# A two-layer spectral convolution on one core: image reloads, sums, differences and inverse adds at other places of the order, and forward stores in half as many transfers

## The reference

```python
# layer 0: real spectrum, one real block weight per channel block of 48
f  = fft2(x, axes=(1, 2), norm='ortho');  Xh = (f.real - f.imag)[:, :, :46]
o2 = relu(Xk @ w1[0] + b1[0]) @ w2[0] + b2[0]          # kept: 23 columns kw
x  = ifft2(pad(softshrink(o2, 0.01)), s=(45, 90)).real + x
# layer 1: complex spectrum, complex block weights
xs = rfft2(x)[:, :, :23];  xr, xi = xs.real, xs.imag
o1r = relu(xr @ w1[0] - xi @ w1[1] + b1[0]); o1i = relu(xi @ w1[0] + xr @ w1[1] + b1[1])
o2r, o2i = softshrink(o1r @ w2[0] - o1i @ w2[1] + b2[0]), softshrink(o1i @ w2[0] + o1r @ w2[1] + b2[1])
y  = irfft2(pad(o2r + 1j * o2i), s=(45, 90)) + x
```

## Time and profile before

| | |
|---|---|
| three runs | 593.26, 598.96, 599.08 us; median 598.96 |
| the profiled execution | 594.54 us, of it 592.6 us from the first to the last instruction (the span) |
| mean granted TensorE clock | 0.947 of full speed |
| PE, DVE, POOL, ACT busy | 81%, 61%, 47%, 36% of the span |
| 16 DMA engines | 108.29 MB, mean 183 GB/s; 73% of their time on the three queues of SP, POOL and ACT |

### The profile page before, as it was taken

The page is one execution under the profiler, slowest core; times in us unless marked ns, Lnnn a source line. Parts: engine busy times, 40 slices in busy tenths (PEclk is TensorE's granted clock), DMA queues, the critical chain, the costliest instruction groups (busy, mean ns, idle before and its releaser), DMA issues.

```text
span 592.6 us, 16944 instructions
## 1 busy us (share of the span) xinstructions
PE 479.6 (81%) x6944; PEld 334.2 (56%) x6944; DVE 361.8 (61%) x728; ACT 211.1 (36%) x485; POOL 276.7 (47%) x267
## 2 busy tenths in 40 slices
PE   1418789998898899798888899699997899997763
PEld 0015568776575667476566566566675666775411
DVE  6625456686576667475747656656776767666532
ACT  1203344544234433253234333254334433443101
POOL 9916542661456424671357523674258522322123
PEclk9999789999998999898997989989999999999958
DMA  8659966364897959794796938968698967633587
GB/s 179 209 115 156 210 150 169 100 176 119 226 239 150 236 144 245 210 219 136 205 256 146 243 100 207 255 151 223 168 236 206 222 188 186 165 106 100 129 222 207
DMA packets 81617, 108.29 MB, mean 183 GB/s; under 512 B 10441, under 2 KB 67903, under 8 KB 81414
## 3 DMA queue, kind: packets, MB, share of 16 engines
q1 hardware_dynamic: 64044, 61.01, 37.7%
q0 software_dynamic: 11024, 40.46, 30.0%
q10 hardware_dynamic: 6474, 5.76, 5.0%
HBM read 53.97 MB, written 53.19 MB: 181 GB/s over the span
## 4 chain that ended last, share of the span: by engine, by line
PE 41%; DMA 24%; DVE 14%; POOL 10%; issue 5%; ACT 2%; SPq 2%; POOLq 0%; DVEq 0%; ACTq 0%
DMA img<-x 20%; PE ps L718 8%; PE ps L667 6%; PE ps L705 6%; PE ps L743 6%; PE ps L624 5%; PE ps L654 5%; DVE img L595 4%; DVE uv L517 4%; POOL y L419 3%; POOL xs L397 3%; DVE ns L571 3%; SPq L327 2%; DMA jr<-scr_i 2%; ACT p L486 2%
## 5 line engine op out<-in xcount | busy, mean ns | idle before, releaser
L411 POOL TENSOR_TENSOR uv<-img 128x768 f32<-128x768 f32 (+1 forms) x48 | 101.6, 2128 | 29.9 <-DMA img<-x 29.5
L419 POOL DMA_DIRECT2D y<-img x56 | 40.1, 718 | 138.7 <-DVE img L595 134.5
L654 PE MATMUL ps<-jr,cst 64*64 64x384 f32 (+1 forms) x736 | 83.7, 518 | 13.8 <-DVE img L595 8.0
L718 PE MATMUL ps<-wt,o 128*64 128x96 f32 x1472 | 78.7, 258 | 19.7 <-DVE o L563 19.3
L667 PEld LDWEIGHTS ps<-cst,bt 128*64 128x64 f32 x1472 | 65.6, 148 | 39.1 <-issue 26.2
L718 PEld LDWEIGHTS ps<-wt,o 128*64 128x64 f32 x1472 | 69.3, 143 | 32.4 <-issue 32.4
L517 DVE TENSOR_TENSOR uv<-img 128x768 f32<-128x768 f32 (+1 forms) x48 | 63.2, 1316 | 37.7 <-DMA img<-x 35.2
L667 PE MATMUL ps<-cst,bt 128*64 128x90 f32 x1472 | 74.5, 259 | 13.8 <-DMA bt<-scr_f 13.8
L595 DVE TENSOR_TENSOR img<-ps,img 109x768 f32<-109x768 f32 x76 | 72.5, 955 | 20.9 <-PE ps L654 20.2
L397 POOL TENSOR_TENSOR xs<-xs,nt 128x360 f32<-128x360 f32 (+1 forms) x48 | 41.6, 867 | 87.3 <-DVE nt L549 66.1
L705 PE MATMUL ps<-xs,wt 64*97 64x180 f32 (+1 forms) x768 | 70.5, 321 | 12.0 <-POOL xs L397 11.7
(11 more groups left out here) (44 smaller groups left out, 456.2 us busy)
## 6 DMA issues: line engine op xcount, KB each, us to landing
y<-img POOLq DMA_DIRECT2D x28, 540.0 KB, 8.0
scr_f<-fs SPq DMA_DIRECT2D x384, 36.0 KB
scr_i<-et SPq DMA_DIRECT2D x48, 288.0 KB, 5.1
jr<-scr_i SPq DMA_DIRECT2D x92, 144.0 KB, 5.7
img<-x POOLq DMA_DIRECT2D x24, 540.0 KB, 9.9
bt<-scr_f SPq DMA_DIRECT2D x40, 288.0 KB, 6.6
y<-img POOLq DMA_DIRECT2D x14, 270.0 KB, 6.8
img<-x POOLq DMA_DIRECT2D x12, 270.0 KB, 5.4
```

The source lines that it names most:

```text
L411: nc.gpsimd.tensor_tensor(uv[n % 2][:, 1, 0:j1 - j0, :], img[t % IMGS][:, j0:j1, 0, :], img[t % IMGS][:, j0:j1, 1, :], ALU.subtract).then_ ...
L654: last = mm(ps[64 * p:64 * p + 64, B0 + a, 0:m], w_inv[c, r, :], set_rows(t, g)[c, p, 0:m], start=True, stop=True)
L718: last = mm(ps[64 * r:64 * r + 64, P2 + p, b * 2 * BS:(b + 1) * 2 * BS], o11[:, b, 2 * p + r, :], w21[:, block_no(s // STEPS, b), :], star ...
```

## The change

The list of `schedule()` is written anew, and the forward part of task 0 is treated apart:

1. **Refills**, in the list of a step before: refill 0 and 1 behind `d0` (steps 5 and 0), refill 2 behind `rows`, refill 3 at the end of step 1. Now: refill 0 and 1 ahead of `d1` and `d0`, refill 2 behind `e` in step 1, refill 3 where refill 2 was.
2. **Sums and differences** (`uv`) come one place later: the first of a step behind `c1`, the second behind `c0`, none at the end of the step before.
3. **Inverse groups** were spread 2, 3, 4 and 3 over steps 3, 4, 5 and 0; the first one now stands at the end of step 2, and steps 3, 4, 5 and 0 have 3 each (after it 1 + 2 in step 3). Chunk 0 ends with group 3, now early in step 4.
4. **The add** of a group is a part of its own. For the group between `d1` and `d0` it stands behind `d0` now, so DVE shrinks layer 0 first. The store of a finished chunk hangs on the add.
5. **Forward stores**: 4 transfers of 72 KB a group in place of 8 of 36 KB, behind both copies.
6. **Forward groups of task 0** use all eight PSUM banks in turn, and DVE copies one of the two banks.

```diff
-            inv[s] = [("inv", t - 1, g) for g in ((0, 1), (2, 3, 4), (5, 6, 7, 8))[i - 3]]
+            inv[s] = [("inv", t - 1, g) for g in ((1, 2), (3, 4, 5), (6, 7, 8))[i - 3]]
+        if i == 2 and 0 < t < TASKS - 1:
+            inv[s] = [None, None, ("inv", t - 1, 0)]
...
-        order += first
+        order += uv[0:1]
+        order += both(groups[0])
         if s > 1:
             order.append(("e", s - 2))
-        order += uv[1:2]
-        order += last[0:1]
+        if i == 1 and t > 1:
+            order.append(("refill", t - 2, 2))
+        order += both(groups[1])
         if s < NSTEPS:
             order.append(("c0", s))
-        if 0 < s <= NSTEPS:
-            order.append(("d1", s - 1))
-        order += last[1:2]
-        if s < NSTEPS:
-            order.append(("d0", s))
+        order += uv[1:2]
         if i == 5 and t > 0:
             order.append(("refill", t - 1, 0))
         if i == 0 and t > 1:
             order.append(("refill", t - 2, 1))
+        if 0 < s <= NSTEPS:
+            order.append(("d1", s - 1))
+        order += both(groups[2])[0:1]
+        if s < NSTEPS:
+            order.append(("d0", s))
+        order += both(groups[2])[1:2]
...
         if i == 1 and t > 1:
-            order.append(("refill", t - 2, 2))
+            order.append(("refill", t - 2, 3))
...
-        order += last[2:3]
-        order += ahead[0:1]
-        if i == 1 and t > 1:
-            order.append(("refill", t - 2, 3))
+        order += both(groups[3])
...
-                    for p in range(2):
-                        sp.wait_ge(f_cp, 2 * n + p + 1)
-                        for a in range(2):
-                            for o in range(2):
-                                sp.dma_start(scr_f[t][o * KWP // 2:(o + 1) * KWP // 2, :, p, g, a].rearrange("k e s c -> (k e) (s c)"),
-                                             fs[k][64 * a + 32 * o:64 * a + 32 * o + KWP, p, :]).then_inc(f_st[k], 16)
+                    sp.wait_ge(*(f_cp, 2 * (n - CH + 1)) if t else (f_act, n + 1))
+                    if t == 0:
+                        sp.wait_ge(f_dve, n + 1)
+                    for a in range(2):
+                        for o in range(2):
+                            sp.dma_start(scr_f[t][o * KWP // 2:(o + 1) * KWP // 2, :, :, g, a].rearrange("k e p s c -> (k e) p (s c)"),
+                                         fs[k][64 * a + 32 * o:64 * a + 32 * o + KWP]).then_inc(f_st[k], 16)
...
+                if kind == "fwd" and what[0] == 0:
+                    g = what[1]
+                    if g >= FS:
+                        dve.wait_ge(f_st[g % FS], 64 * (g // FS))
+                    dve.wait_ge(f_mm, g + 1)
+                    nc.vector.tensor_copy(fs[g % FS][:, 1, :], ps[:, 2 * (g % 4) + 1, 0:2 * HC]).then_inc(f_dve, 1)
...
-                if kind == "inv" and (what[0] < TASKS - 1 or what[1] not in LAST_POOL):
+                if kind == "add" and (what[0] < TASKS - 1 or what[1] not in LAST_POOL):
```

More of the change, by code:

```diff
@@ L120, in schedule, with both @@
 def schedule():
+    def both(group):
+        return [group, ("add",) + group[1:]] if group else []
     order = [("uv", 0, 0), ("uv", 0, 1)]
@@ L141, in schedule @@
         t, i = divmod(s, STEPS)
-        first, last = inv[s][0:len(inv[s]) - 3] if len(inv[s]) > 3 else [], inv[s][max(len(inv[s]) - 3, 0):]
+        groups = [None] * (4 - max(len(inv[s]), 3)) + inv[s]
+        groups += [None] * (4 - len(groups))
         uv = [("uv",) + f[1:] for f in fwd[s]]
-        ahead = [("uv",) + f[1:] for f in fwd[s + 1]] if s + 1 < NSTEPS else []
         if s + 2 < NSTEPS:
@@ L364, in _ @@
                                      scr_i[t][:, :, a, 4 * j:4 * j + 4, :].rearrange("k e h c -> (k e) (h c)")).then_inc(landed, 16)
-                if kind == "inv" and what[0] == TASKS - 1 and what[1] % 2 == 1:
+                if kind == "add" and what[0] == TASKS - 1 and what[1] % 2 == 1:
                     g, (b, f) = what[1] // 2, divmod(TASKS - 1, HALVES)
@@ L412, in _ @@
                                             ALU.subtract).then_inc(v_ok, 1)
-                if kind == "inv" and what[0] < TASKS - 1 and (what[1] + 1) // 2 in [b for a, b in CHUNKS] and what[1] % 2 == 1:
+                if kind == "add" and what[0] < TASKS - 1 and (what[1] + 1) // 2 in [b for a, b in CHUNKS] and what[1] % 2 == 1:
                     t, g = what
@@ L426, in _ @@
                         pool.dma_start(folded(k, p, j0, j1), rows_of(x[b], HR * p + j0, HR * p + j1, f)).then_inc(x_ld[k][c], 16)
-                if kind == "inv" and what[0] == TASKS - 1 and what[1] in LAST_POOL:
+                if kind == "add" and what[0] == TASKS - 1 and what[1] in LAST_POOL:
                     t, (g, r) = what[0], divmod(what[1], 2)
@@ L448, in _ @@
                     if n >= FS:
[L449 removed]
+                        act.wait_ge(f_st[n % FS], 64 * (n // FS))
                     act.wait_ge(f_mm, n + 1)
[L451 to L452 removed]
+                    if t == 0:
+                        nc.scalar.activation(fs[n % FS][:, 0, :], ps[:, 2 * (g % 4), 0:2 * HC], ACT.Copy).then_inc(f_act, 1)
+                    else:
+                        for p in range(2):
+                            nc.scalar.activation(fs[n % FS][:, p, :], ps[:, P3 + p, 0:2 * HC], ACT.Copy).then_inc(f_cp, 1)
                 if kind == "x":
@@ L627, in _ @@
                     for p in range(2):
[L628 removed]
+                        tenant[p] = [(f_cp, 2 * (n - CH) + p + 1)] if t else []
                 if kind == "inv":
```

25 lines of the change are left out of this document (15 added, 10 removed).

## The result

| | before | changed |
|---|---|---|
| median of four runs each | 596.11 us | 619.66 us |
| lowest to highest | 592.52 to 599.08 | 615.47 to 622.20 |
| profiled execution / its span | 594.54 / 592.6 us | 615.47 / 613.7 us |
| mean granted TensorE clock | 0.947 | 0.939 |

The ratio is 1.039, 95% interval 1.029 to 1.049. The forecast was 587 us with a range of 571 to 604: wrong in sign. All ratios in this text leave disturbed runs out on both sides, so a ratio can differ by up to 1.2% from that of the medians beside it. Single runs of one kernel lie within 1.1% of each other in the table; in the later sets of 13 runs the kernel before lies as far apart as 584.5 and 603.9 us.

A forecast was written before the change was run, and what follows sets the result against it. The bound was taken as a full PE with two reload waits a cycle. From 594.5 us, -6 at the start, -5 in tasks 0 and 1 and +3 over five cycles gave 586.5, rounded 587; range 571 to 604.

The forecast's parts named there:

- Third stretch: Third step of a task cycle, 14.92 us before: 9.4 us plus W plus 1.7 us of half clock.
- W: New wait a cycle: refill 1 on POOL waits for chunk 1's store, holding `c1` and PE; 6.5 us taken.
- first rival: The wait for the store is short, 3.3 us a cycle: 571 us, chance 0.22.
- Fourth stretch: Fourth step of a cycle: as before at 8.9 us, put at 9.1 to allow for POOL.
- First stretch: First step of a cycle, 11.02 us before: loses one inverse group and its rests of 1.17 us, leaving 9.0.
- Fifth stretch: Fifth step of a cycle: three inverse groups, and 2.1 us of rest from the add behind `d0`; 13.5 us in all.
- The start: Task 0's forward stores, 24 issues for 48 on SP: first load at 30.5 us against 36.46, -6.
- third rival: The start gives nothing, by doubled issue cost or a fourth group waiting for DMA: 593 us, chance 0.12.
- Tasks 0 and 1: Ahead of the cycles: earlier `c1` and `d1`, and a late load's wait gone; -5 us, bounds -1 and -9.
- one us more: Part of the term for tasks 0 and 1: one us more at the first sum.
- The end: Behind the cycles, without refills or forward groups: only adds trade places, 0 us.
- slow rival: Refill wait grows to 9 us and the first inverse group waits 2 us for `jr`: 616 us, chance 0.14.

The follow-up runs named there:

- b_refills: The kernel before with all four refills at their new places and nothing else: 609.09 us, ratio 1.028.
- u_refill01: The changed kernel with refills 0 and 1 both back behind `d0`: 596.10 us, ratio 1.009.
- narrow difference: The changed kernel with POOL's differences over one of four row slots, so output is not the reference's: one run, 603.99 us.
- c_late: `c_add3` with the store of chunk 0 issued behind `d0` of step 4, behind SP's load of the next task: 589.99 us, ratio 0.989.
- u_add3: The changed kernel with only the add of step 3 back ahead of `d0`: 610.68 us, ratio 1.022.
- c_late_act: `c_late` with two of the four forward stores of each group of task 0 issued by ACT: 588.66 us, ratio 1.000.
- c_add3: The changed kernel with refills 0 and 1, sums and differences, and the add of step 3 at their former places: 588.36 us, ratio 0.987.

## Why the prediction was wrong, step by step

- **Third stretch: right.** Predicted 17.6 with W = 6.5, was 16.7 with 5.85 us of rest, 5.5 of it ahead of `c1`. The place, the mechanism and the half clock behind it were as written; POOL's wait for stores, 20 to 35 us in the text, was 67.2, because refill 0 waits too. I had granted refill 0 a landed store. The first rival, a short wait, is out. As forecast, no sum waits for an image in the cycles any more. The step had this wait paid back by the waits that it takes away, in the stretches below; they were not free of rest, and `b_refills` and `u_refill01` put the price of the early refills at about 3%.
- **Fourth stretch, "9.1 to allow for POOL": the largest miss, 2.3 us a cycle, 11 in all.** The prediction counted the moved sum at its own duration. It did not ask what POOL does at that moment. With refill 3 moved away from between them, two differences stand back to back in POOL's order, and the sum of DVE stands beside both. The narrow difference shows that the sum is long by them. That refill 3's new place brings them together is read from the order and the rows; no run undid it alone. The runs with that new place, other than the narrow one, have fourth stretches of 10.2 to 14.9 us, the kernel before 9.1. A rule of the Trainium skill bears on this, "SBUF — State Buffer", section "Who interferes with whom": a DVE instruction with two inputs in SBUF contends with a GpSimd instruction that reads SBUF, over a pair of ports that is an exclusive lock. The trace agrees that the sum is held up: it began 0.82 us behind the first of two differences of 1.82 us and ended at 264.48, 0.82 us behind their end at 263.66, where a sum alone takes 0.94. It did not get its turn between the two, though it had begun by then.
- **First stretch, 9.0: 1.7 us a cycle too little, 8.5 in all.** The rest was counted as gone with DVE's and POOL's late work; 0.4 of it stayed. The other 1.3 stand ahead of `a`: moving the inverse groups moved the store of chunk 0 from just behind the load of the next task to just ahead of it, and the load landed with the store. `c_late` shows this last step by turning the two round. That the moved groups set the order is read from the trace: no run undid them alone, and in `b_refills`, which has them at the old place, the store also came first in two cycles of five (loads of 11.8 and 10.6 us). It never came up among the rivals: the third step of the change was read for PE's and DVE's work, and the DMA that hangs on an add was followed to its refill only.
- **Fifth stretch, 13.5: was 14.4.** The rest that the late add makes was 2.29 us for 2.1 forecast; 0.56 more stands ahead of the first inverse group. `u_add3` gets 1.0 us of it back.
- **The start, -6: was -1.** This is the third rival. The lower bound, "a transfer of twice the bytes takes twice the issue", was the truth. The loads of 288 KB, taken as a sign against it, are of another form. `c_late_act` shows that issue did bind, and that taking half of the stores off SP gave 2.8 and not 6.
- **Tasks 0 and 1, -5: was 0.** The terms do not add up to 5 as they stand: 3 and 2.2 with "one us more" are 6.2, or 4.2 if it is a cost. The 2.2, a load that SP issued late and that I counted as gone with half the issues, stayed: PE rests 2.22 us ahead of the cycles' first `a` (2.21 before), as the issues were no shorter. The add, priced at "nothing net" here, cost 1.25 in step 3 of task 1 (a rest of 2.29 for 1.04). In task 0 two executions of the same order differ by 2 to 3 us, so the rest of this term cannot be told from spread.
- **The end, 0: was -1.8.** Within the spread.

In sum: cycles +23.6 for +3, start and tasks 0 and 1 together -0.8 for -11. The slow rival (616 us) came near in time, but not by its mechanism: at the new first inverse group, in the fifth stretch, PE rests 0.56 us a cycle, and by the profile this ends with ACT's copy out of the PSUM bank and not with the landing of `jr`.

On the one rule weighed beforehand: with the Trainium skill's "DMA: Bandwidth & Descriptors", section on the anatomy of one DMA from GpSimd (2.0 us plus bytes / 436e3, an estimated 3.3 us for 540 KB), POOL would hardly have waited. The page of the changed kernel has these stores at 9.9 us in the median (8.0 before), and the runs decide against that figure here.

**Left open.** Why the third stretch's gain from undoing refill 1 alone (3.0 us) came back by half in the fourth (1.6) was not followed further. Undone one by one, refills, sums and add give back 3.0, 1.4 and 1.7%, which is more than the loss of 3.9%; how they depend on each other is not shown. The new places of refills 2 and 3 and of the inverse groups were never undone alone. Whether any version beats the kernel before by more than the spread is not settled: `c_add3` stands at 0.987 (0.978 to 0.995), its successors `c_late` at 0.989 (0.979 to 1.000) and `c_late_act` at 1.000 (0.992 to 1.007). By the medians of all runs the three are at 0.992, 0.990 and 0.988.

## What to carry to other kernels

Here the landing of a load went by what had been issued just before it on another queue. When work is moved, list the DMAs that hang on it and ask for each what it now stands ahead of: a store of 1 MB issued 1.35 us ahead of a 0.3 MB load in place of 0.34 us behind it moved that load's landing by 7 us. And look at what a moved instruction stood between: with the refill gone from between them, two differences of POOL ran back to back, and the sum of DVE beside them was held up by both. Last, undo the parts of a change together as well as one by one; here the single gains did not add.

## What the runs showed of the hardware

- The first load of a task (288 KB, issued by SP) against a store of two transfers of 540 KB on POOL's queue, in the five cycles of all kernels: it lands 3.1 to 3.5 us behind its issue when the second transfer goes 0.46 us or more behind it; 6.3 to 7.3 us when the second goes between 0.36 us ahead and 0.30 us behind; 9.4 to 11.8 us when the first has gone 1.3 to 2.4 us ahead and the second 0.5 us or more; and 4.5 to 7.1 us when the first has gone 4.8 to 6.3 us ahead. A reload 1.4 to 2.2 us ahead does the same as such a store (9.9 to 10.9).
- SP's issue of a forward store goes by its pieces: in the median 0.76 us for 48 of 1.5 KB, 0.37 for 24. A load of 288 KB takes 0.3 us at the least and 0.5 in the median.
- In the cycles of the changed kernel a DVE sum of two SBUF tiles (128x768) takes 0.94 us alone, 1.7 to 2.6 beside one POOL difference and 2.6 to 4.2 beside two back to back, in the mean 3.5. In `c_add3` one of 5.05 us began 0.63 us ahead of the first of two differences, beside POOL's issue of a refill.
- The first transfer of a store of chunk 0 lands 5.6 to 7.4 us behind its issue, the second 8.8 to 12.3. The second of chunk 1 lands 11.9 to 14.1 in the changed kernel, where a refill is issued ahead of it, and 9.7 to 10.8 in the kernel before.
